# A decoder block in fp32: row 0's stacks loaded by half heads, transfers reordered, and the odd rows' gate and projection matmuls dealt out

## The reference

```python
x = x + pos_emb[:S][None]                                   # x: the layernorm of the input
w = xp.reshape(B, nW, WIN, H, hd)                           # windows of 128
attn = softmax(einsum("bnqhd,bnkhd->bhnqk", w, w) * scale)  # local attention
local = einsum("bhnqk,bnkhd->bnqhd", attn, w)
comp = conv(x, conv_w, stride 4) + conv_b                   # 64 compressed tokens of the row
gt = concat([comp, global_memory])                          # with 64 global ones: 128
glob = einsum("bhsg,bghd->bshd", softmax(einsum("bshd,bghd->bhsg", x, gt) * scale), gt)
mix = sigmoid(concat([local, glob]) @ gate_w + gate_b)
out = (mix * local + (1.0 - mix) * glob) @ out_w + out_b
```

## Time and profile before

| | us |
|---|---|
| median of 3 runs (lowest, highest) | 1112.37 (1111.96, 1116.95) |
| the profiled execution, its own time | 1110.8 |
| its span, first to last instruction | 1109.0 |
| PE busy | 1060.6 (96%) |
| DVE / ACT / POOL busy | 668.6 / 646.8 / 555.9 |
| self-attention, about | 0 to 435 |
| cross-attention and experts | 435 to 1109 |

### The profile page before, as it was taken

The page is one execution under the profiler, slowest core; times in us unless marked ns, Lnnn a source line. Parts: engine busy times, 40 slices in busy tenths (PEclk is TensorE's granted clock), DMA queues, the critical chain, the costliest instruction groups (busy, mean ns, idle before and its releaser), DMA issues.

```text
span 1109.0 us, 28590 instructions
## 1 busy us (share of the span) xinstructions
PE 1060.6 (96%) x11089; PEld 914.7 (82%) x11089; DVE 668.6 (60%) x1318; ACT 646.8 (58%) x873; POOL 555.9 (50%) x678
## 2 busy tenths in 40 slices
PE   7899999999999998999999998999999999999996
PEld 7777777777877776777778777899999999999995
DVE  4587888888888878788888887323424222222221
ACT  2456666565666666787777876454454444444441
POOL 6455355463535233433666566477744444444442
PEclk9999999999999999999999999999999999999998
DMA  8663644636454523666676568765432333233222
GB/s 215 170 185 105 169 125 112 171 93 170 112 142 124 144 82 76 175 171 175 143 162 173 143 173 261 202 110 57 45 55 44 53 48 49 49 48 49 48 44 24
DMA packets 174562, 130.22 MB, mean 117 GB/s; under 512 B 60810, under 2 KB 162927, under 8 KB 174432
## 3 DMA queue, kind: packets, MB, share of 16 engines
q1 hardware_dynamic: 155280, 106.79, 36.2%
q0 software_dynamic: 15840, 18.77, 11.8%
q10 hardware_dynamic: 3312, 2.85, 0.9%
HBM read 88.29 MB, written 40.08 MB: 116 GB/s over the span
## 4 chain that ended last, share of the span: by engine, by line
PE 55%; DVE 2%; ACT 1%; issue 1%; DMA 1%; POOLq 0%; ACTq 0%
PE ps_scores L1991 23%; PE ps_out L2026 11%; PE ps_turn L1854 5%; PE ps_misc L1886 3%; PE ps_out L1866 2%; PE ps_scores L1841 2%; PE ps_misc L1807 2%; PE ps_misc L1874 2%; PE ps_turn L1970 1%; PE ps_scores L1834 1%; PE ps_scores L1915 1%; PE ps_misc L1880 1%; PE ps_turn L1896 1%; ACT weights L2199 1%; DMA out<-y,out_row 1%
## 5 line engine op out<-in xcount | busy, mean ns | idle before, releaser
L1991 PEld LDWEIGHTS ps_scores<-xgT,weights 128*128 128x128 f32 x2240 | 260.3, 192 | 3.3
L1991 PE MATMUL ps_scores<-xgT,weights 128*128 128x128 f32 x2240 | 262.0, 275 | 0.0
L2508 DVE TENSOR_TENSOR gate<-ps_scores,silu 128x512 f32<-128x512 f32 x70 | 48.4, 691 | 237.5 <-ACT silu L2239 237.5
L960 ACT ACTIVATE weights<-ps_scores 128x1024 f32<-128x1024 f32 x128 | 126.8, 1023 | 76.8 <-PE ps_scores L632 61.3
L2239 ACT ACTIVATE silu<-ps_scores 128x512 f32<-128x512 f32 x70 | 41.8, 597 | 198.3 <-PE ps_scores L1991 198.2
L2026 PE MATMUL ps_out<-w2s,gate 128*128 x552 | 130.6, 379 | 0.0
L2232 ACT COPY weights<-weights 128x2048 f32 x68 | 129.9, 1910 | 0.2
L2026 PEld LDWEIGHTS ps_out<-w2s,gate 128*128 128x128 f32 x552 | 99.5, 190 | 10.7
L1133 DVE TENSOR_REDUCE sa_rowmax<-ps_turn 128x8 bf16<-128x1024 f32 x64 | 77.7, 1215 | 34.0 <-PE ps_turn L609 34.0
L965 ACT CAST weights<-ps_scores 8x1024 bf16<-8x1024 f32 x64 | 64.3, 1005 | 51.3 <-PE ps_scores L623 51.3
L1701 POOL DMA_INDIRECT xg<-xn_rows,slot_row x71 | 70.5, 993 | 25.1 <-issue 19.7
(11 more groups left out here) (332 smaller groups left out, 2123.4 us busy)
## 6 DMA issues: line engine op xcount, KB each, us to landing
weights<-w_scr SPq DMA_DIRECT2D x60, 256.0 KB, 3.9
weights<-q_scr SPq DMA_DIRECT2D x96, 128.0 KB
ks<-w_scr SPq DMA_DIRECT2D x24, 256.0 KB, 3.9
weights<-k_scr SPq DMA_DIRECT2D x48, 120.0 KB
w_scr<-wp SPq DMA_DIRECT2D x7, 768.0 KB, 3.9
q_scr<-qp SPq DMA_DIRECT2D x14, 384.0 KB, 3.6
weights<-in_w1T SPq DMA_DIRECT2D x10, 512.0 KB, 6.6
weights<-in_w3T SPq DMA_DIRECT2D x10, 512.0 KB, 8.6
```

Source lines behind the costliest of these rows:

```text
L960: act.activation(probs[s % 2][:], m.scores[s % 2][:], ACT.Exp, scale=SCALE).then_inc(exped, 1)
L1991: mm = pe.matmul(h_ps[r % 2][:, j, c, :], weights[:, j, k, c * P:(c + 1) * P], xgT[r % 2][:, k, :], start=(k == 0), stop=(k == DT - 1))
```

## The change

- Row 0's stacks are loaded by half heads f: 24 DMAs instead of 12, those of f = 0 first. `scores(0, 0)` waits for f = 0 alone, `scores(0, 2)` for f = 1. The tokens of row 0 are loaded by halves too (12 instead of 6), f = 0 by ACT.
- The tokens of pair 0 are split by DVE instead of POOL and stored from ACT's queue; PE's `turn_g(0)` and ACT's copies of it go ahead of those for the context. `g_scr` is laid out so that a partition's two pieces are adjacent: runs of 768 B instead of 384 B in the store.
- Row 1's store follows row 0's stacks and tokens on SP. `gate_w` comes behind row 1's query stack, x and context of the next pair amid its key stack, `out_b` and `out_w` after `store_w(1)` and `store_keys_values(1)`. The token store of pair 1 stands amid the key stack of rows 2 and 3, its load straight behind it.
- POOL's first four `add_out_bias` move from row 0 to row 1.
- In odd rows `turn_g` writes to `side[1]` (half of `m.turn`) instead of `m.misc`, so the gate for o = 0 can start there: matmul 0 behind `turn_g`, 1 and 2 in the old place, 3 behind `turn_max(b, 3)`, with `squash` moved behind it. `project` is cut in two, the first half ahead of `values(b, 5)`.
- The counts of `keep_warm` are 6, 12, 4, 5, 14, 22, 5 instead of 14, 8, 4, 7, 16, 34, 3.

The diff, without the bodies of `split_first_g` (the three ops of `split_g`, on DVE) and `ones_of_g` (the copy that DVE made for both `gs` in a loop):

```diff
...
     w_scr = [nc.dram_tensor(f"w_scr{i}", [3, D, R * S], BF16, kind="Internal").ap() for i in range(2)]
-    g_scr = [nc.dram_tensor(f"g_scr{i}", [3, D, GK], BF16, kind="Internal").ap() for i in range(2)]
+    g_scr = [nc.dram_tensor(f"g_scr{i}", [3, P, DT, GK], BF16, kind="Internal").ap() for i in range(2)]
...
-    N_FIRST, N_CONV, N_REST = 2 * 16, 4 * 16, 5 * 16
+    N_FIRST, N_CONV, N_REST = 2 * 16, 4 * 16, 3 * 16
...
+    def load_first_heads(queue, f, dst, scratch, parts, loaded, slots):
         for s in slots:
...
+            queue.dma_start(dst[s:KS:SLOTS, f * HU:(f + 1) * HU, :],
+                            scratch[parts[s], f * P:(f + 1) * P, :].rearrange("(h d) t -> d h t", d=HD))\
+                .then_inc(loaded(s), 16)
+
+    def load_first_tokens(queue, f, loaded, slots):
+        for s in slots:
+            queue.dma_start(gs[0][s:KS:SLOTS, f * HU:(f + 1) * HU, :],
+                            g_scr[0][K_PARTS[s], :, f, :].rearrange("(h d) t -> d h t", d=HD)).then_inc(loaded(s), 16)
...
     first_row = w_scr[0][:, :, 0:S]
+    first_qs, first_ks = qs[0][:, :, 0, :], ks[0][:, :, 0, :]
+    heads_of_row0 = lambda f: lambda s: row0_stacked[f]
+    heads_of_g = lambda f: lambda s: g_stacked[s % 3] if f else row0_stacked[2]
+    FIRST_HEADS, FIRST_GLOBAL = 2 * SLOTS * 16, SLOTS * 16
...
     def sync_program(sp):
...
-        def stack(dst, scratch, parts, loaded, before, under_way, paced=True):
+        def stack(dst, scratch, parts, loaded, before, under_way, amid=None):
...
             for s, part in enumerate(parts):
-                if paced and (s > 2 or under_way):
+                if s == 3 and amid is not None:
+                    amid()
+                if s > 2 or under_way:
...
+        def load_pair():
+            load_x(2)
+            load_ctx(2)
...
         def stack_second_row():
...
             stack(qs[0][:, :, 1, :], rows, Q_PARTS, w_stacked, 0, False)
-            stack(ks[0][:, :, 1, :], rows, K_PARTS, w_stacked, 32, True)
...
+            sp.dma_start(gate_w[:], a["gate_w"].rearrange("(k p) o -> p k o", p=P)).then_inc(rest_in, 16)
+            stack(ks[0][:, :, 1, :], rows, K_PARTS, w_stacked, 32, True, amid=load_pair)
+
+        def store_w(p):
+            i = p % 2
+            sp.wait_ge(w_split, 3 * R * (p + 1))
+            if p > 1:
+                for loaded in w_stacked:
+                    sp.wait_ge(loaded, 64 * p)
+            sp.dma_start(w_scr[i].rearrange("c (k p) t -> p c k t", p=P), wp[:].rearrange("p c k r t -> p c k (r t)"))\
+                .then_inc(w_stored, 16)
...
         def stack_w(p):
             i = p % 2
-            sp.wait_ge(w_split, 3 * R * (p + 1))
...
                 sp.wait_ge(loaded, 64 * p)
-            sp.dma_start(w_scr[i].rearrange("c (k p) t -> p c k t", p=P), wp[:].rearrange("p c k r t -> p c k (r t)"))\
-                .then_inc(w_stored, 16)
...
             stack(qs[i].rearrange("k h r t -> k h (r t)"), w_scr[i], Q_PARTS, w_stacked, 64 * p, False)
-            stack(ks[i].rearrange("k h r t -> k h (r t)"), w_scr[i], K_PARTS, w_stacked, 64 * p + 32, True)
+            stack(ks[i].rearrange("k h r t -> k h (r t)"), w_scr[i], K_PARTS, w_stacked, 64 * p + 32, True,
+                  amid=(lambda: store_g(p)) if p == 1 else None)
...
         def store_g(p):
...
                     sp.wait_ge(loaded, 32 * p)
-            sp.dma_start(g_scr[i].rearrange("c (k p) t -> p c k t", p=P), gp[:]).then_inc(g_stored, 16)
+            sp.dma_start(g_scr[i].rearrange("c p k t -> p c k t"), gp[:]).then_inc(g_stored, 16)
...
         def load_g(p):
...
                 sp.wait_ge(shifted, R * UPR * (p - 1))
-            stack(gs[i][:], g_scr[i], K_PARTS, g_stacked, 32 * p, False)
+            for s, part in enumerate(K_PARTS):
+                if s > 2:
+                    sp.wait_ge(g_stacked[s % 3], 32 * p + 16)
+                sp.dma_start(gs[i][s:KS:SLOTS].rearrange("d (k h) t -> d k h t", k=DT),
+                             g_scr[i][part].rearrange("(h d) k t -> d k h t", d=HD)).then_inc(g_stacked[s % 3], 16)
...
         store_first_pair(0, row0_stored)
-        stack_first_row()
+        sp.wait_ge(row0_stored, 16)
+        load_first_heads(sp, 0, first_qs, first_row, Q_PARTS, heads_of_row0(0), range(SLOTS))
+        load_first_heads(sp, 0, first_ks, first_row, K_PARTS, heads_of_row0(0), range(3, SLOTS))
+        load_first_heads(sp, 1, first_qs, first_row, Q_PARTS, heads_of_row0(1), range(SLOTS))
+        load_first_heads(sp, 1, first_ks, first_row, K_PARTS, heads_of_row0(1), range(4))
+        sp.wait_ge(g_stored, 16)
+        load_first_tokens(sp, 1, heads_of_g(1), range(3))
         store_first_pair(1, w_stored)
-        store_g(0)
-        load_first_g()
-        sp.dma_start(gate_w[:], a["gate_w"].rearrange("(k p) o -> p k o", p=P)).then_inc(rest_in, 16)
-        sp.dma_start(out_b[:], a["out_b"].unsqueeze(0).broadcast_to((P, D))).then_inc(rest_in, 16)
-        sp.dma_start(out_w[:], a["out_w"].rearrange("(k p) o -> p k o", p=P)).then_inc(rest_in, 16)
+        store_keys_values(0)
         stack_second_row()
-        store_keys_values(0)
-        load_ctx(2)
+        store_w(1)
+        store_keys_values(1)
+        sp.dma_start(out_b[:], a["out_b"].unsqueeze(0).broadcast_to((P, D))).then_inc(kv_in, 16)
+        sp.dma_start(out_w[:], a["out_w"].rearrange("(k p) o -> p k o", p=P)).then_inc(kv_in, 16)
         for p in range(1, NP):
-            if p < NP - 1:
+            if 1 < p < NP - 1:
                 load_x(p + 1)
+            if p > 1:
+                store_w(p)
             stack_w(p)
-            store_g(p)
-            store_keys_values(R * p - 1)
+            if p > 1:
+                store_g(p)
+                store_keys_values(R * p - 1)
+            else:
+                load_g(p)
             load_ctx(R * p + 1)
-            load_g(p)
+            if p > 1:
+                load_g(p)
...
         deviations(2)
-        split_g(0)
...
                 difference(b - 1)
+            if b == 1:
+                pool.wait_ge(kv_in, 4 * 16)
+                for c in range(4):
+                    add_out_bias(c)
...
                 pool.tensor_scalar(gate_b[:], gate_b[:], 0.5, None, ALU.mult).then_inc(bias_set, 1)
-                for c in range(3):
-                    add_out_bias(c)
-            if ahead:
+            elif ahead:
...
+        def turn_g(p, bank):
...
         def scores(b, s):
...
             i = p % 2
-            if s == 0 and b == 0:
-                for loaded in row0_stacked:
-                    pe.wait_ge(loaded, 64)
+            if b == 0 and s in (0, 2):
+                pe.wait_ge(row0_stacked[f], FIRST_HEADS)
...
             i = p % 2
-            if s == 1:
+            if b == 0 and s == 1:
+                pe.wait_ge(row0_stacked[2], FIRST_GLOBAL)
+            elif s == (1 if b else 3):
...
-        def gate(b, o):
-
-            if b + o == 0:
+        def gate_part(b, o, parts):
+            if b + o == 0 and parts[0] == 0:
                 pe.wait_ge(rest_in, N_REST)
-            for i, c in enumerate((0, 2, 1, 3)):
+            for i in parts:
+                c = (0, 2, 1, 3)[i]
...
+            if parts[-1] == 2 * DT - 1:
+                mm.then_inc(gate_made, 1)
+
+        def gate(b, o):
+            gate_part(b, o, range(2 * DT))
+
+        def project_rows(b, n):
+            if b + n == 0:
+                pe.wait_ge(kv_in, 4 * 16)
+            pe.wait_ge(mixed, b + 1)
+            for k in range(DT):
+                mm = pe.matmul(proj_place(b)[:, n * D:(n + 1) * D], mixT[:, k, n * P:(n + 1) * P], out_w[:, k, :],
+                               start=(k == 0), stop=(k == DT - 1))
+            if n == NT - 1:
+                mm.then_inc(proj_made, 1)
...
         pe.wait_ge(first_in, N_FIRST)
-        keep_warm(14)
+        keep_warm(6)
         turn_w(0, m.misc)
-        keep_warm(8)
+        keep_warm(12)
...
             compress(0, k)
+        turn_g(0, m.misc)
         turn_c(0, whole_out)
-        turn_g(0)
-        keep_warm(7)
+        keep_warm(5)
...
         pe.wait_ge(dve_set, 1)
-        keep_warm(16)
+        keep_warm(14)
         scores(0, 0)
-        keep_warm(34)
+        keep_warm(22)
...
             if not old:
-                keep_warm(3)
+                keep_warm(5)
...
                 else:
-                    turn_g(p + 1)
+                    turn_g(p + 1, side[1])
+                    gate_part(b - 1, 0, range(1))
...
+            if nxt and not even:
+                pe.wait_ge(gT_read, p + 2)
...
                     pe.wait_ge(wT_read, b + 3)
-                elif nxt:
-                    pe.wait_ge(gT_read, p + 2)
...
                     pe.wait_ge(m.q_read, 2)
-                gate(b - 1, 0)
+                if nxt and not even:
+                    gate_part(b - 1, 0, range(1, 2 * DT - 1))
+                else:
+                    gate(b - 1, 0)
...
                 turn_w(b + 3, side[1])
+            elif nxt:
```

(34 more changed lines are left out.)

37 lines of the change are left out of this document (13 added, 24 removed).

## The result

The median of 12 runs is 1108.14 us (1105.03 to 1110.95), that of 12 runs of the kernel before, made beside them, 1114.52 (1110.91 to 1117.19): a ratio of 0.9942, with an interval of 0.9929 to 0.9956, so 6.4 us or 0.6% faster. The forecast was 1101.8, a ratio of 0.9905, and its range ended at 1107.5. The profiled execution took 1108.45 (span 1106.6), 2.35 less than that of before.

The account below looks back on a forecast made before the run. The tokens were taken to bound the start, PE (busy 320 of 335 us) the later rows. 5.0 + 1.1 - 0.3 + 0.9 + 3.85 = 10.55 us off 1110.8, plus 1.6 for the median, gave 1101.8; range 1097.0 to 1107.5.

Parts of the forecast that it names:

- The start: Up to the first query scores: earlier tokens bring `queries_scores(0, 1)` to 31.0 from 36.09, 5.0 us less.
- Rival 3: Row 0's stacks: a halved transfer costs the engines what a whole one does, the start gains nothing; 1106.9, chance 0.07.
- Rival 4: Start: PE's clock rises later, so the start gains 3.4 us; 1103.4, chance 0.08, counted within the forecast's 0.52.
- Rival 5: Row 0: tokens land late, PE idles after its shortened warming and the clock falls; 1122, chance 0.05.
- Row 0: Keys stored ahead of row 1's stack and POOL's adds moved to row 1: 1.1 us less.
- Rows 1 and 2: the transfers moved: SP's reordered transfers land in time, and PE's idle at row 2's first `queries_scores` goes: 0.9 us less.
- The odd rows: Gate matmuls put into PE's gaps: 0.55 us less in each of 7 odd rows, 3.85 in all.
- the projection's half: End of odd rows: splitting the projection saves PE 0.5 us, not paid because PE waits for DVE.
- DVE's closed run: Odd row's end: DVE is busy without a gap from unit 7's maximum through `residual`, and starts only 0.55 us earlier.
- Rival 1: Odd rows pay nothing, because tokens or DVE take all of the gain; 1105.7, chance 0.17.
- Rival 2: Odd rows pay in full, the projection's half too, if DVE's run gets shorter; 1098.2, chance 0.12.
- The tokens of even rows: Next to be late: half a us to spare, used up by the 0.55; a shorter store gives about 0.5 back.

Follow-up runs that it names:

- experiment 6: Changed kernel with row 0's stacks loaded by 12 whole transfers again instead of 24 halves, the tokens still by halves; 1107.48 us, ratio 0.9969.
- Experiment 2: Changed kernel with SP's queue from row 1's store on in the order of the kernel before; ratio 0.9992.
- experiment 7: Changed kernel with `out_b` and `out_w` loaded by ACT in the first microseconds, behind `wv`; 1102.52 us, ratio 0.9913.
- Experiment 9: Changed kernel with the odd rows' projection whole at the row's end again, the gate still dealt out; 1107.13 us, ratio 0.9951.
- experiments 10: Kernel of experiment 7 with POOL's `add_out_bias` ahead of `split_k` in odd rows; 1100.81 us, ratio 0.9909.
- experiment 12: Kernel of experiment 10 with all six loads of `gs` issued at once, without waiting for the first three; 1098.35 us, ratio 0.9882.
- experiment 11: Kernel of experiment 10 with the odd rows' projection whole, as in experiment 9; 1101.97 us, ratio 0.9914.

## Why the prediction was right or wrong

**The start** (5.0 forecast): right in its path, with terms that cancel. PE's first query scores came 4.81 earlier, at 31.28 for 31.0, the first exponential 4.50. But `gn` came no earlier than before (18.56 for 18.60; I had reckoned 0.4), the token store was issued at 21.62 for 21.3 and took 3.9 us, not 3.4; that is 0.8 too late at the loads, and the last load then landed 2.4 us after its issue instead of 2.9. Rival 3 (halves cost as wholes) is refuted by the first halves, at 25.36. Rival 4 is refuted by PE's matmuls: 7 in the microsecond from 8 us, 8 in the next, 12 from 10 on (6, 9 and 11 before). Rival 5 didn't happen here, row 0 has no fall; in experiment 6 it did, for 3.4 us and 1.5 us of row 0. Its price of 1122 was a slip, the 9.5 us added to the kernel before and not to the forecast.

**Row 0** (1.1): 0.87, for the two reasons given. Experiment 2 shows the first of them at its worst.

**Rows 1 and 2: the transfers moved.** This is the step that failed. I reckoned that the stack would land near 68.5 against a need of 71.9, and the tokens by 74, with `gs` no longer last, and took 0.9 off. The stack landed at 76.1 and the tokens at 81.9, and rows 1 and 2 came 5.9 longer instead. The term that was wrong is the stack's time: 14 us and 2 for `store_g(1)`, from a store landed at 52.5. The 7.6 us between 68.5 and 76.1 are made up so. The store landed 1.5 later, at 54.0. The 14 us were the stretch of the issues of before (58.08 to 72.09), not the time to the last landing, which was 17.5 us even there; in experiment 7, where `out_b` and `out_w` are out of the way, it is 19.7 with `store_g(1)` amid, so 3.7 of the 7.6 are this. And I had named what follows `store_w(1)` but gave its 804 KB no time of their own: with the 384 KB of `out_b` and `out_w` ahead it took 22.0 instead of 19.7, which makes the last 2.4. That is also why experiment 7 keeps waits of 0.4 and 1.7 at row 2. The earlier trace rows had shown both: `scores(0, 0)` waited for its loads until 28.00, 6.1 us after SP's last issue had ended, and a token store behind other transfers took 5.5. Then there was a second price that I had nothing for at this place, the clock: 1.4 us in row 2. Rival 5 had the mechanism, a late transfer and a clock that falls, but put it in row 0.

**The odd rows** (0.55 each): right, 0.57 a pair, though by 1.2 less in odd rows and 0.66 more in even ones: 21.29 for the 22.0 forecast, 26.52 for 25.9. Experiment 9 shows that the projection's half isn't paid, and that its cut is what moves this 0.65 from odd to even rows (21.94 and 25.88 without it). That it is DVE's closed run that sets the pair's end fits its unchanged 5.57 us and experiments 10 and 12, but isn't the whole of it: in experiment 11, with the divide at 0.43 and hardly a wait for tokens, a pair is 0.2 less than in 9, not 0.5. Rival 1 gave nearly the measured time (0.9942 of 1112.37 is 1105.9) by a mechanism that didn't happen; a time alone doesn't confirm a rival. Rival 2's rate, 1.0 a pair, is reached (47.29 for 48.38) in experiment 12, with two more edits: the divide undisturbed and the tokens unpaced. The tokens of even rows were named as next, "just enough". It wasn't quite: PE waits for them at two even rows of the changed kernel (0.6 and 1.0), and experiments 10 and 12 show that they are next.

**What stays open:** why the wait at row 2 differs from run to run (0.5 and 1.0 in one kernel's profile, 2.4 and 3.1 in another's with the same order of transfers, whose query slots took 7.8 and 10.4 us) was not tried; what of row 1's time the clock has, beside the 1.4 in row 2; whether the unpaced tokens would pay without the other edits.
